# Second expert matmul in three rounded float32 terms, with the parts made on ScalarE and GpSimd

## The chip, the cores and the metric

The kernel runs on one core of a Trainium2 chip. The metric is the time of one execution on the device in microseconds (us), as a median over runs. A profiled execution leaves a page and a trace; every time in this text comes from them or from the runs.

## What is computed

A transformer layer on x of shape (16, 512, 128) in float32: layer norm, block-sparse attention and a residual, then layer norm, a mixture of four experts of which each row uses two, and a residual. The part that changes is the second matmul of the experts:

```python
h = jax.nn.gelu(jnp.einsum('nd,edh->enh', xf, w1) + b1[:, None, :], approximate=False)
y = jnp.einsum('enh,ehd->end', h, w2) + b2[:, None, :]
out = jnp.einsum('nk,nkd->nd', gates, y_sel - c_sel + c_sum[None, None, :])
```

The attention picks blocks by data: for each block of 64 queries and each head, the own block of keys and the best other one.

## The kernel before, in words

**Sizes.** B = 16 batch items, each one "batch" here. N = 512 rows, D = 128, H = 16 heads, M = 8 blocks of BS = 64 queries, E = 4 experts of C = 4 chunks of 128 hidden units, so UPS = 16 chunks per batch.

**Stages and their overlap.** The order of every engine is written out by hand; the engines meet by semaphores alone. Each batch b has a loop over m = 0 to 7, in which the attention of batch b runs. Between its steps stand the projections for batch b+1 (`a_columns`, `project`, `a_products`), the routing of batch b-1 (`c_columns`, `c_route`, `c_gates`) and the second expert matmul of batch b-2: two `c_down` per m on TensorE (L379 to L388), one between `row_max` and `shift`, one behind the next scores. After the loop come the 16 first expert matmuls `c_up` of batch b-1 (L363 to L377), each in three rounded terms (`exact`, L246 to L249, of types float32r), with the Gelu on ScalarE (L876 to L883) that fills `hid`. Behind k = 13 (`UP_SPREAD`) stands `begin(b+1)`, the scores and values of m = 0 of the next batch. Batch 15 has a tail without attention, in which 32 `c_down` and 16 `c_up` follow each other.

**An attention step m.** TensorE: `weighted(m-1)` (L322), `row_max(m)` (L306), `c_down`, `shift(m)` (L314), `scores(m+1)` (L279, line L295), `c_down`, `values(m+1)`. VectorE: `row_max` makes `nmax` (L618), for which `shift` waits; `block_max` (L603, line L609) makes `rmax` from the scores, for which `row_max` waits. ScalarE: `shift_exp` (L847), for which `weighted` waits; `values` makes `vaug` (L840).

**The selection.** At m = 6, VectorE's `a_select(b+1)` (L585 to L601) makes `index`, in ten short steps that wait for each other, the last of them L600. It stands right behind `row_max(6)` and ahead of `block_max(7)` (L764). GpSimd's `a_select` (L941, line L947) gathers with it by an indirect DMA. SP then issues `put_selected` (L1035), `put_gates`, five `place_q`, and `take_selected` (L1039, line L1044), which loads the chosen keys and values into kv. `scores(b+1, 0)` waits for its landing (`sel_in`, L285).

**GpSimd besides.** Reciprocal roots (`inverse`), `a_rows` (L938), `c_split` (L953), and `c_sum` (L967), which adds the gated experts. VectorE's `c_gated` (L705) multiplies an expert's result with its gate column; there are NG = 4 gate buffers, one for each expert, filled by SP's `take_gate` (L1056).

The f32 matmul of one `c_down` is one line, which the chip runs as two instructions:

```python
pe.wait_ge(gelued, UPS * b + n + 1)
ins = pe.matmul(dst[:], w2s[:, n, :], hid[:, n, :], start=(c == 0), stop=(c == C - 1))
```

## Time and profile before

| | us |
|---|---|
| median of 3 runs (lowest, highest) | 1009.13 (1005.77, 1011.89) |
| the profiled execution, its own time | 1008.49 |
| its span, first to last instruction | 1006.9 |
| TensorE busy (share, instructions) | 932.7 (93%, 9572) |
| VectorE busy | 552.1 (55%) |
| ScalarE busy | 460.2 (46%) |
| GpSimd busy | 172.6 (17%) |
| y_ps from hid and w2s, L386, 480 records | 260.8 busy, 629 ns each |
| first term of `exact` on w1, L247, 256 | 112.2 busy, 438 ns each |
| `block_max`, L609, 256 | 167.8 busy, 693 ns each |
| Gelu, L883, 256 | 171.5 busy, 688 ns each |

How to read it: the granted clock of TensorE is full from about 150 us on, and mostly half of it before, where the first two batches stand with gaps. Records of consecutive matmuls overlap (their ends are modelled), so a step's true length is read from start to start in the timeline and not from the mean. An average over the whole span hides what ends last in one step; the order of the steps around m = 6 and around k = 13 has to be read in the timeline.

### The profile page before, as it was taken

How to read it: one execution, taken by the hardware profiler on the slowest of the kernel's cores; microseconds unless marked ns; L12 is line 12 of the kernel's file. 1: busy time of each engine (PE TensorE's matmuls, PEld its weight loads, DVE VectorE, ACT ScalarE, POOL GpSimd, SP SyncE). 2: the span in 40 equal slices, each digit the busy share in tenths (PEclk: the TensorE clock that was granted, in tenths of full speed). 3: DMA queues.
4: the chain of work that ended last, by engine and by line, in shares of the span. 5: the costliest groups of instructions: out<-in, count | busy, mean ns of one | idle time of the engine just before them, and what ended most of it. 6: DMA issues, size and time to landing. Idle time of an engine off the chain costs nothing.

```text
span 1006.9 us, 24099 instructions
## 1 busy us (share of the span) xinstructions
PE 932.7 (93%) x9572; PEld 599.8 (60%) x9572; DVE 552.1 (55%) x1555; ACT 460.2 (46%) x740; POOL 172.6 (17%) x174
## 2 busy tenths in 40 slices
PE   3584889999999999999999999999999999999996
PEld 2362666575666666565666556566666656665652
DVE  6262645747475655747474565746575665734321
ACT  1131345363735445373635436363645436363641
POOL 3120101121212121120212121111212121110221
PEclk8575679999999999999999999999999999999998
DMA  7424052342506243352515344251615334250110
GB/s 208 115 70 120 4 142 88 109 135 72 164 14 177 63 138 103 96 147 61 164 26 150 88 123 119 76 168 36 176 38 140 99 114 119 74 159 2 54 51 14
DMA packets 96819, 101.06 MB, mean 100 GB/s; under 512 B 8744, under 2 KB 83376, under 8 KB 96688
## 3 DMA queue, kind: packets, MB, share of 16 engines
q1 hardware_dynamic: 94400, 86.89, 30.9%
q0 software_dynamic: 2304, 12.58, 3.9%
q8 instruction: 78, 1.28, 0.5%
q14 instruction: 37, 0.30, 0.1%
HBM read 48.98 MB, written 29.49 MB: 78 GB/s over the span
## 4 chain that ended last, share of the span: by engine, by line
PE 67%; DVE 17%; issue 6%; ACT 4%; SPq 3%; DMA 2%; POOL 0%; POOLq 0%; DVEq 0%
PE y_ps L386 15%; PE s_ps L295 10%; PE s_ps L318 6%; DVE rmax L609 6%; PE o_ps L329 5%; PE s_ps L247 5%; PE s_ps L249 5%; PE s_ps L248 5%; ACT hid L883 4%; SPq L1032 3%; PE v_ps L304 2%; DVE gate_cols L705 2%; PE o_ps L336 2%; PE a_ps L256 2%; PE a_ps L359 1%
## 5 line engine op out<-in xcount | busy, mean ns | idle before, releaser
L386 PE MATMUL y_ps<-hid,w2s 128*128 128x512 f32 x480 | 260.8, 629 | 0.8 <-DVE yT L705 0.2
L609 DVE TRANSPOSE_TENSOR_REDUCE rmax<-s_ps 128x16 bf16<-128x512 f32 x256 | 167.8, 693 | 165.6 <-PE s_ps L295 165.6
L847 ACT ACTIVATE prob<-s_ps 128x1024 f32<-128x1024 f32 x128 | 131.2, 1025 | 201.0 <-PE s_ps L318 200.8
L883 ACT ACTIVATE hid<-s_ps,b1s 128x512 f32<-128x512 f32 x256 | 171.5, 688 | 37.1 <-PE s_ps L249 35.4
L295 PE MATMUL s_ps<-qdiag,kv 64*128 64x512 f32 x768 | 138.2, 467 | 19.2 <-DMA kv<-kv_chosen 18.2
L840 ACT COPY vaug<-v_ps 128x128 f32<-128x128 f32 x128 | 34.0, 265 | 205.6 <-PE v_ps L304 205.6
L318 PEld LDWEIGHTS s_ps<-nmax,hone 16*128 16x128 bf16 x2048 | 69.7, 95 | 97.6 <-DVE nmax L618 96.6
L247 PE MATMUL s_ps<-xnhi,w1hi 128*128 128x512 f32 x256 | 112.2, 438 | 1.4
L967 POOL TENSOR_TENSOR yT<-yT,gate_cols 128x512 f32<-128x512 f32 x48 | 61.4, 1279 | 283.2 <-DVE gate_cols L705 282.8
L295 PEld LDWEIGHTS s_ps<-qdiag,kv 64*128 64x128 f32 x768 | 86.6, 256 | 35.2 <-issue 27.4
L248 PE MATMUL s_ps<-xnlo,w1hi 128*128 128x512 f32 x256 | 101.2, 395 | 0.0
L249 PE MATMUL s_ps<-xnhi,w1lo 128*128 128x512 f32 x256 | 101.2, 395 | 0.0
L386 PEld LDWEIGHTS y_ps<-hid,w2s 128*128 128x128 f32 x480 | 73.7, 190 | 37.7 <-issue 22.9
L318 PE MATMUL s_ps<-nmax,hone 16*128 16x64 bf16 x2048 | 85.2, 192 | 8.0 <-DVE nmax L618 5.8
L329 PE MATMUL o_ps<-prob,vaug 128*32 128x64 f32 x4096 | 88.4, 229 | 3.3 <-ACT prob L847 1.4
L329 PEld LDWEIGHTS o_ps<-prob,vaug 128*32 128x32 f32 x4096 | 67.8, 114 | 38.5 <-issue 23.9
L618 DVE TENSOR_REDUCE nmax<-v_ps 16x64 bf16<-16x256 bf16 x128 | 52.4, 409 | 69.4 <-PE v_ps L311 69.4
L247 PEld LDWEIGHTS s_ps<-xnhi,w1hi 128*128 128x128 f32 x256 | 50.1, 196 | 17.7 <-ACT hid L883 8.8
L304 PEld LDWEIGHTS v_ps<-idn,kv 128*128 128x128 f32 x128 | 24.6, 192 | 57.2 <-DVE x L637 30.7
L855 ACT COPY oT<-o_ps 128x512 f32<-128x512 f32 x64 | 37.5, 586 | 41.2 <-PE o_ps L329 40.8
L249 PEld LDWEIGHTS s_ps<-xnhi,w1lo 128*128 128x128 f32 x256 | 48.3, 189 | 11.7
L705 DVE SCALAR_TENSOR_TENSOR gate_cols<-y_ps,mT,gate_cols 128x512 f32<-128x512 f32 x45 | 32.6, 724 | 41.2 <-PE y_ps L386 41.2
(139 smaller groups left out, 1079.1 us busy)
## 6 DMA issues: line engine op xcount, KB each, us to landing
gate_cols<-gates SPq DMA_DIRECT2D x64, 256.0 KB, 5.2
kv_table<-stage SPq DMA_DIRECT2D x16, 768.0 KB, 3.9
kv<-stage SPq DMA_DIRECT2D x16, 768.0 KB, 6.2
kv_chosen<-selected SPq DMA_DIRECT2D x16, 768.0 KB, 5.3
kv<-kv_chosen SPq DMA_DIRECT2D x16, 768.0 KB, 4.9
qdiag<-qpair SPq DMA_DIRECT2D x512, 16.0 KB
xs<-in_x SPq DMA_DIRECT2D x16, 256.0 KB, 4.5
out_x<-x SPq DMA_DIRECT2D x16, 256.0 KB, 4.6
```

The costliest lines, as they stand in the source:

```text
L247: pe.matmul(dst, left_hi, right_hi, start=True, stop=False)
L248: pe.matmul(dst, left_hi, right_lo, start=False, stop=False)
L249: return pe.matmul(dst, left_lo, right_hi, start=False, stop=True)
L295: ins = pe.matmul(s_ps[i][:, half * N:(half + 1) * N].rearrange("p (h s) -> p h s", s=BS), keys, queries, start=n == 0, stop=False, skip_g ...
L318: ins = pe.matmul(s_ps[i][:, h * BS:(h + 1) * BS], hone[:, h, :], nmax[i][:], start=False, stop=True, skip_group_check=True)
L329: ins = pe.matmul(o_ps[32 * (h % HQ):32 * (h % HQ) + VW, h // HQ, i * BS:(i + 1) * BS], vaug[i][:, h, :], prob[i][:, h, :], start=True, st ...
L386: ins = pe.matmul(dst[:], w2s[:, n, :], hid[:, n, :], start=(c == 0), stop=(c == C - 1))
L609: v.tensor_reduce(rmax[m % 2][:, half * 8:(half + 1) * 8, :], s_ps[m % 2][:, half * N:(half + 1) * N].rearrange("p (a c) -> p a c", c=32), ...
L705: v.scalar_tensor_tensor(dst[:], src[:], mT[:, e:e + 1], gate_cols[i][:], ALU.add, ALU.mult).then_inc(of.free, 1)
L847: act.activation(prob[m % 2][:].rearrange("p h s -> p (h s)"), s_ps[m % 2][:], ACT.Exp, scale=SCALE).then_inc(exped, 1)
L883: act.activation(hid[:, k, :], up_ps[up_bank(k)], ACT.Gelu, bias=b1s[:, k:k + 1]).then_inc(gelued, 1)
L967: g.tensor_tensor(yT[:], yT[:], gate_cols[(E * b + e) % NG][:], ALU.add).then_inc(summed, 1)
```

## The change

The second expert matmul is computed like the first. w2 is split once into a rounded high part and a low part (`w2hi`, `w2lo`), on GpSimd, in batch 0. Each Gelu chunk gets a high part (`c_hi`: on ScalarE for n = 2 to 15, on GpSimd for n = 0, 1 and in the tail) and a low part (`c_lo`: a subtraction, on GpSimd, in the tail on VectorE). Two buffers of each serve in the loop, so a cast waits for the `c_down` two before it (`weighed_of`); in the tail eight places in `qdiag` serve. `c_down` issues three matmuls. Two gate buffers are left of four, and the gates of experts 2 and 3 are taken one batch later in SP's queue. `a_select` moves to the end of m = 6 on VectorE, and on GpSimd between two `c_lo`. The core of the diff, in the order of the file: declarations, then TensorE, VectorE, ScalarE, GpSimd (its `c_lo` uses `g`) and SP.

```diff
-        w2s = sb("w2s", [P, E * C, D])
+        w2hi, w2lo = sb("w2hi", [P, E * C, D], F32R), sb("w2lo", [P, E * C, D], F32R)
...
-        NX, N2, NG = 3, 3, E
+        NX, N2, NH, NG = 3, 3, 2, 2
...
+        hidhi, hidlo = ([sb(f"hid{part}{i}", [P, N], F32R) for i in range(NH)] for part in ("hi", "lo"))
...
-                pe.wait_ge(gelued, UPS * b + n + 1)
-                ins = pe.matmul(dst[:], w2s[:, n, :], hid[:, n, :], start=(c == 0), stop=(c == C - 1))
-                if c == C - 1:
-                    ins.then_inc(of.full, 1)
+                if b == 0 and n == 0:
+                    pe.wait_ge(w_split, SPLIT_W2)
+                pe.wait_ge(*low_of(b, n))
+                pe.matmul(dst[:], w2hi[:, n, :], hi, start=(c == 0), stop=False)
+                pe.matmul(dst[:], w2lo[:, n, :], hi, start=False, stop=False)
+                ins = pe.matmul(dst[:], w2hi[:, n, :], lo, start=False, stop=(c == C - 1))
+                ins.then_inc(of.full if c == C - 1 else weighed, 1)
...
+            def c_lo(b, n):
+                hi, lo, _ = parts_of(b, n)
+                v.wait_ge(*high_of(b, n))
+                v.tensor_tensor(lo, hid[:, n, :], hi.bitcast(F32), ALU.subtract).then_inc(lo_done, 1)
...
-                        if m == 6:
-                            tied = a_select(b + 1)
                     if b >= 1:
                         if m == 1:
                             c_route(b - 1)
...
                     if b >= 1 and m == 5:
                         c_split(b - 1)
+                    if b + 1 < B and m == 6:
+                        tied = a_select(b + 1)
                     if b >= 1 and m == 6:
                         c_gates_turned(b - 1)
...
             c_add(b - 1)
             c_gated(b, 0)
             for e in range(1, E):
+                c_los(b, e * C, (e + 1) * C)
                 c_gated(b, e)
...
+            def c_hi(b, n):
+                hi, _, was = parts_of(b, n)
+                act.wait_ge(*weighed_of(was))
+                act.copy(hi, hid[:, n, :]).then_inc(hi_cast, 1)
...
+                    if b >= 2 and m + 1 < M:
+                        c_hi(b - 2, 2 * m + 2)
                     if m in (3, 5, 7):
                         o_columns(b, (m - 3) // 2)
...
+                    if b >= 2 and m + 1 < M:
+                        c_hi(b - 2, 2 * m + 3)
                 o_copy(b, T - 1)
...
+            def c_lo(b, n):
+                hi, lo, _ = parts_of(b, n)
+                g.wait_ge(*high_of(b, n))
+                g.tensor_tensor(lo, hid[:, n, :], hi.bitcast(F32), ALU.subtract).then_inc(lo_pooled, 1)
...
+                    if b >= 2 and m in (4, 6):
+                        c_sum(b - 2, m // 2 - 1)
                     if b + 1 < B:
                         if m == 0:
                             inverse(b + 1, mv, veps, rstd, mean_done, rstd_done)
                         if m == 1:
                             a_rows(b + 1)
-                        if m == 6:
-                            a_select(b + 1)
-                    if b == 0 and m < E:
-                        split_w1(m)
+                    if b == 0:
+                        split_w(m)
+                    if b >= 2 and m + 1 < M:
+                        c_lo(b - 2, 2 * m + 2)
                     if b >= 1 and m == 5:
                         c_split(b - 1)
-                    if b >= 2 and m in (4, 6):
-                        c_sum(b - 2, m // 2 - 1)
+                    if b + 1 < B and m == 6:
+                        a_select(b + 1)
+                    if b >= 2 and m + 1 < M:
+                        c_lo(b - 2, 2 * m + 3)
                 if b >= 2:
                     c_sum(b - 2, E - 1)
+                if b >= 1:
+                    for n in range(NH):
+                        c_hi(b - 1, n)
+                    for n in range(NH):
+                        c_lo(b - 1, n)
                 inverse(b, mv2, veps2, rstd2, mean2_done, rstd2_done)
...
+                if b >= 2:
+                    take_gate(b - 2, 2)
                 if b + 1 < B:
                     place_q(b + 1, 0, range(8))
+                if b >= 2:
+                    take_gate(b - 2, 3)
                 if b + 1 < B:
                     a_v(b + 1, bank_a, bank_a)
...
```

In the tail GpSimd makes the high parts in groups (`c_his`) between its sums, and VectorE the low parts (`c_los`) between its other steps, those of an expert ahead of its `c_gated`.

## Rows read from the trace of the kernel before

**Rows 1.** Busy time of each engine in 500 to 600 us (windows view), with granted clock.

```profile
500.00:600.00 100.00, 97.85 (x1097) 61.20 (x1096) 62.81 (x174) 44.66 (x74) 17.49 (x17) 1.00 0.34 96
```

**Rows 2.** Timeline (start, length, engine, line, operation): selection chain up to the scores.

```profile
493.00 0.38 SPq L1044 DMA_DIRECT2D kv<-kv_chosen  x1
...
498.55 1.03 PE L295 MATMUL s_ps<-qdiag,kv 64*128 64x512 f32 x6
...
537.94 1.10 POOL L947 DMA_INDIRECT selected<-kv_table,index  x1 [1.79 <-DVE index L600]
...
543.69 0.59 SPq L1037 DMA_DIRECT2D kv_chosen<-selected  x1
...
550.75 0.38 SPq L1044 DMA_DIRECT2D kv<-kv_chosen  x1
...
556.37 1.03 PE L295 MATMUL s_ps<-qdiag,kv 64*128 64x512 f32 x6 [0.83 <-ACT hid L883]
```

**Rows 3.** Timeline of TensorE in the loop: two downs, and three rounded terms.

```profile
506.79 1.12 PE L386 MATMUL y_ps<-hid,w2s 128*128 128x512 f32 x2
507.84 0.64 PE L318 MATMUL s_ps<-nmax,hone 16*128 16x64 bf16 x16
...
509.91 1.13 PE L386 MATMUL y_ps<-hid,w2s 128*128 128x512 f32 x2
510.87 0.27 PE L304 MATMUL v_ps<-idn,kv 128*128 128x128 f32 x1
...
521.59 0.48 PE L247 MATMUL a_ps<-xnhi,wqkvhi 128*128 128x512 f32 x1
521.91 0.39 PE L248 MATMUL a_ps<-xnlo,wqkvhi 128*128 128x512 f32 x1
522.14 0.40 PE L249 MATMUL a_ps<-xnhi,wqkvlo 128*128 128x512 f32 x1
522.47 0.65 PE L329 MATMUL o_ps<-prob,vaug 128*32 128x64 f32 x32
```

**Rows 4.** Timeline of TensorE in the tail: the downs of two experts.

```profile
989.02 3.60 PE L386 MATMUL v_ps<-hid,w2s 128*128 128x512 f32 x8
...
992.45 3.60 PE L386 MATMUL y_ps<-hid,w2s 128*128 128x512 f32 x8
```

**Rows 5.** Timeline of TensorE, m = 6 to m = 7 of one batch.

```profile
535.59 0.64 PE L318 MATMUL s_ps<-nmax,hone 16*128 16x64 bf16 x16
536.15 1.03 PE L295 MATMUL s_ps<-qdiag,kv 64*128 64x512 f32 x6
...
541.39 0.64 PE L318 MATMUL s_ps<-nmax,hone 16*128 16x64 bf16 x16
...
543.14 0.65 PE L329 MATMUL o_ps<-prob,vaug 128*32 128x64 f32 x32
```

**Rows 6.** Groups of instructions by form: a copy on ScalarE, a subtraction on GpSimd.

```profile
L855 ACT COPY oT<-o_ps 128x512 f32<-128x512 f32 x64 | 37.5, 586 | 41.2 <-PE o_ps L329 40.8
...
L953 POOL TENSOR_TENSOR xnlo<-xn2T,xnhi 128x512 fp32r<-128x512 f32 x16 | 20.2, 1263 | 181.6 <-DVE xnhi L654 181.6
```

**Rows 7.** Timeline at m = 6, GpSimd and VectorE; last, all L591 (ns min/median/max).

```profile
534.89 1.26 POOL L953 TENSOR_TENSOR xnlo<-xn2T,xnhi 128x512 fp32r<-128x512 f32 x1 [10.89 <-DVE xnhi L654]
...
535.29 0.94 DVE L591 TENSOR_TENSOR crow<-crow,mine_of 128x64 f32<-128x64 f32 x1
...
537.44 0.21 DVE L600 TENSOR_SCALAR index<-cbest,rbase 128x1 uint32<-128x1 f32 x1
537.57 1.30 DVE L609 TRANSPOSE_TENSOR_REDUCE rmax<-s_ps 128x16 bf16<-128x512 f32 x2
...
539.25 0.29 DVE L628 TENSOR_TENSOR att<-o_ps,rden 128x128 f32<-128x128 f32 x1
...
L591 DVE TENSOR_TENSOR crow<-crow,mine_of x16: 224/934/940, 17.2 to 877.8; 128x64 f32<-128x64 f32 x16
```

**Rows 8.** Timeline of TensorE: the first scores of batch 1.

```profile
92.84 1.65 PE L295 MATMUL s_ps<-qdiag,kv 64*128 64x512 f32 x6 [9.29 <-DMA kv<-kv_chosen]
```

More of the change, by code:

```diff
@@ L243, in bank_of, with parts_of, high_of, low_of @@
             return next(of for of, _ in banks.values() if use in of.at)
+        TAIL, NT = UPS * (B - 2) + 2, 8
+        def parts_of(b, n):
+            at = UPS * b + n
+            if at < TAIL:
+                return hidhi[at % NH][:], hidlo[at % NH][:], at - NH
+            i = (at - TAIL) % NT
+            hi, lo = (q[:, i // 4, i % 4 * 2:i % 4 * 2 + 2, :].rearrange("p h s -> p (h s)") for q in qdiag)
+            return hi, lo, at - NT if at - NT >= TAIL else None
+        def high_of(b, n):
+            at = UPS * b + n
+            if at >= TAIL:
+                return hi_moved, NH * (B - 1) + at - TAIL + 1
+            return (hi_moved, NH * b + n + 1) if n < NH else (hi_cast, (UPS - NH) * b + n - NH + 1)
+        def low_of(b, n):
+            at = UPS * b + n
+            return (lo_done, at - TAIL + 1) if at >= TAIL else (lo_pooled, at + 1)
+        def weighed_of(at):
+            b, n = divmod(at, UPS)
+            if n % C == C - 1:
+                of = bank_of("down", b, n // C)
+                return of.full, of.at["down", b, n // C]
+            return weighed, at - at // C + 1
+        SPLIT_W1, SPLIT_W2 = E, 2 * E
         def tensor(pe):
@@ L799, in vector, with c_los @@
             b = B - 1
+            def c_los(b, first, last):
+                for n in range(first, last):
+                    c_lo(b, n)
+            c_los(b - 1, 2, C)
             c_split(b)
+            c_los(b - 1, C, 2 * C)
             c_gated(b - 1, 0)
@@ L982, in pool, with c_his @@
                             a_rows(b + 1)
[L983 to L986 removed]
+                    if b == 0:
+                        split_w(m)
+                    if b >= 2 and m + 1 < M:
+                        c_lo(b - 2, 2 * m + 2)
                     if b >= 1 and m == 5:
                         c_split(b - 1)
[L989 to L990 removed]
+                    if b + 1 < B and m == 6:
+                        a_select(b + 1)
+                    if b >= 2 and m + 1 < M:
+                        c_lo(b - 2, 2 * m + 3)
                 if b >= 2:
                     c_sum(b - 2, E - 1)
+                if b >= 1:
[3 more added lines that the diff above has]
+                        c_lo(b - 1, n)
                 inverse(b, mv2, veps2, rstd2, mean2_done, rstd2_done)
             b = B - 1
+            def c_his(b, first, last):
+                for n in range(first, last):
+                    c_hi(b, n)
+            c_his(b - 1, 2, C)
             c_split(b)
[L996 to L999 removed]
+            c_his(b - 1, C, 3 * C)
+            c_sum(b - 1, 1)
+            c_his(b - 1, 3 * C, 4 * C)
+            c_sum(b - 1, 2)
+            c_his(b, 0, C)
+            c_sum(b - 1, 3)
+            c_his(b, C, 3 * C)
+            c_sum(b, 1)
+            c_his(b, 3 * C, 4 * C)
+            c_sum(b, 2)
+            c_sum(b, 3)
         def sync(s):
@@ L1099, in sync @@
                 if b >= 1:
-                    for e in range(E - 1):
-                        take_gate(b - 1, e)
+                    take_gate(b - 1, 0)
                 if b + 1 < B:
@@ L1104, in sync @@
                 if b >= 1:
-                    take_gate(b - 1, E - 1)
+                    take_gate(b - 1, 1)
             b = B - 1
             store(b - 2)
+            take_gate(b - 1, 2)
+            take_gate(b - 1, 3)
             put_gates(b)
-            for e in range(E):
-                take_gate(b, e)
+            take_gate(b, 0)
+            take_gate(b, 1)
             store(b - 1)
+            take_gate(b, 2)
+            take_gate(b, 3)
             store(b)
```

54 lines of the change are left out of this document (37 added, 17 removed).

## The prediction

> **What bounds the kernel now.** I read the busy time by stretch first. In the steady state, 500 to 600 us, the clock is granted in full (1.00, the 2.4 GHz level), TensorE is busy 97.85 of 100 us, VectorE 62.81, ScalarE 44.66 and GpSimd 17.49 [rows 1]. So TensorE looks like the bound, and shorter expert matmuls look like a gain. Then I read TensorE's own timeline for what one `c_down` takes in place, and the other engines' timelines around m = 6 for what stands next to it. What the reader is to see there: between TensorE's last `shift` steps and the first scores of the next batch runs a second chain that TensorE's busy time hides: block selection on VectorE (`a_select`), gather on GpSimd, `put_selected` and `take_selected` on SP, landing, `scores(b+1, 0)`. In the batch at 537 us it even ends last: the scores at 556.37 stand behind 0.83 us of idle, 5.62 us after `take_selected` was issued at 550.75 [rows 2]. The view names ScalarE's L883 as releaser, but that gelu (k = 13) isn't what this step waits for; the landing of kv is. In the batch before, 493.00 to 498.55 is 5.55 us, without idle [rows 2]. So this chain has between 0 and some 0.6 us of slack; I take 0.4.
>
> **Part 1, three terms in place of one f32 matmul.** A `c_down` in the loop takes 1.05 us to the `shift` behind it (506.79 to 507.84) and 0.96 us to the transpose behind it (509.91 to 510.87) [rows 3]. Three rounded terms of the same shape (128 columns of weights, 512 moving) take 0.32 + 0.23 + 0.33 = 0.88 us, from 521.59 to the next step at 522.47 [rows 3]. So I take 0.88 for the new `c_down`: 0.17 and 0.08 less, nearly 2 us for the 16 of a batch. Back to back, four f32 downs take 3.43 us (989.02 to 992.45) [rows 4], and four triples at 0.23 a term some 2.8, so up to 0.6 for an expert in the tail. Not all of it counts: in m = 2, 4 and 6 VectorE, not the down, sets when `shift` starts, and in m = 7 the exp sets when `weighted` starts: 543.14, 1.75 us after `shift` at 541.39 [rows 5]. I take 1.2 us per batch from the scores of a batch to its `shift(6)`, with ends 0 and 1.9. Batches 2 to 14, 13 of them, are where it meets the selection chain.
>
> **Part 2, the casts on ScalarE.** 14 `c_hi` per batch. The nearest rows are copies and casts of 128x512 from PSUM at 0.586 us [rows 6]: 8.2 us per batch of 57.8 (the scores at 498.55 to those at 556.37 [rows 2]). ScalarE idles over half the time, and each `c_hi` stands where it used to wait for TensorE: behind an exp (that one is over 1.75 us after `shift` starts [rows 5], so the cast some 2.3 us after it) or behind `values`. Its own wait, for the down two before, is satisfied by then. Queued behind it are `attT` and `vaug`; both have a few tenths of a microsecond left. I cost it at 0, at most 0.2 for each of m = 3, 5 (0.4 per batch).
>
> **Part 3, the subtractions on GpSimd.** 16 `c_lo` at 1.263 us (nearest row, the same subtraction in `c_split` [rows 6]) plus two copies, for which no more than that: at most 22.7 us per batch on top of some 10 [rows 1], so 33 of 57.8. Per m that is 2.5 us in some 5.8 (`shift(6)` to `shift(7)` [rows 5]), and a buffer's round (down, cast 0.58, subtraction 1.26) stays under one m. The tight ones by this count are `c_lo(2)`, because exp(0) waits for a table load, and 4, 12, 13 and 14: ready within 0.3 us of their use. Cost 0, at most 0.5 per batch. The exception is `c_lo(15)`, in part 4.
>
> **Part 4, `a_select` moved, on both engines.** This sets the sign. On VectorE it stood behind `row_max(6)` and ends now at 537.65 (537.44 + 0.21), 2.06 us after `shift(6)` at 535.59 [rows 5, 7]. It is moved behind `block_max(7)`, `o_project` and `o_rows`. `block_max(7)` starts now at 537.57, held back by the selection; scores(7) run 536.15 to 537.18 [rows 5], so it can start at about 537.23, 0.34 earlier. The work from its start to the end of L628 is 1.97 us (537.57 to 539.54) [rows 7], which gives 539.2. With one short step ahead of it (0.2 us, my estimate) L591 starts near 539.4, and from the end of L591 to that of L600 it is 1.42 us. L591 takes 0.224 us when alone and 0.934 as median: it ends with `c_split` on GpSimd (534.89 + 1.26 = 536.15, L591 at 536.23) [rows 7]. After the change `c_lo(14)`, started behind `c_lo(13)` and `c_sum`, runs to about 540.05 and holds it the same way. So the index is there at about 541.55, 5.96 us after `shift(6)`: 3.9 us later (3.4 if L591 finds the port free). Everything in the chain follows one to one: gather, 543.69 for `put_selected`, 550.75 for `take_selected`, since SP waits for the gather with nothing else to do and the five `place_q` DMAs between the two are still to be issued behind it. 3.9 less 0.4 of slack: the next batch's scores start 3.5 us later after `shift(6)`.
>
> Beside this, `row_max(7)` on VectorE now queues behind `a_select` and the gate copy: `shift(7)` moves from +5.80 to about +6.6 us. And on GpSimd `c_lo(15)` queues behind the gather, which waits for the index: index + 0.29 + 1.10 [rows 2] + 1.26 is +8.6; `down(15)` follows, and `weighted(7)` behind it starts at +9.5, where it starts at +7.55 now [rows 5]. That is 1.9 us, but inside the 3.5.
>
> The Trainium skill (SBUF — State Buffer, "SBUF: two separate sides") calls the port pair that VectorE and GpSimd share an exclusive lock, held for a whole instruction, against a VectorE instruction with two SBUF inputs. On L591 the trace agrees, 0.224 against 0.934 us. Its page GPSIMD Engine Reference ("Engine selection") speaks against part 3: two-input elementwise work belongs on VectorE, about twice as fast. The sum does without either.
>
> **Part 5, two gate buffers, start and tail.** The takes of gates 2 and 3 move to the next batch's queue on SP, ahead of `place_q` and of `a_v`; what they wait for (`c_gated(0)` and the first `c_sum`) is there by m = 4, before `a_v` can go. Cost 0 to 0.3. Batch 0: TensorE waits 9.29 us for that chain, until 92.84 [rows 8], so nothing of the 3.9 is slack, and the scores ahead of the moved selection are slower, 1.65 us there against 1.03 [rows 5, 8]: 3.9 + 0.6 = +4.5. Batch 1 has more slack and no `c_lo`: +2 (0 to 3.5). The split of w2 on GpSimd (four more pairs, at most 2 x 1.263 us each) ends before anything needs it. In the tail of 32 downs, TensorE gains up to 0.55 per expert, but the high parts go to GpSimd (between 0.6, as ScalarE needs, and 1.26 each) and the low parts to VectorE (some 0.65), in series with `c_gated` in VectorE's queue: the last three experts come out level with now (by my estimate 2.9 for the downs, 0.7 for `c_gated` and 2.5 for four subtractions, where [rows 4] have 3.43 for the downs alone and one expert's gate hidden behind the next). I take +1, from -4 to +5.
>
> **The sum.** 13 x (3.5 - 1.2) = 30; batches 0 and 1 add 6.5; the tail 1: +37.5 on the profiled execution's 1008.5 us (span 1006.9), so 1046. The median of the runs shown is 1009.1, 0.6 higher, well inside the range.
>
> **The rivals.** (a) The chain of DMAs isn't what ends last: the index is later, but SP or the landings give the time back. Then the delay of `shift(7)` and `down(15)` is left, 1.9 us: 13 x (1.9 - 1.2) = 9, with 4.5 + 1 + 1 it is 1024. For it speaks that I have the slack from two batches only; against it the 0.83 us of idle in one of them. (b) The shared port costs more: GpSimd's back-to-back instructions win against a waiting VectorE in `c_gates` (L680, L685 of m = 3), so that `nmax` waits for a whole `c_sum`, and in the tail casts and subtractions alternate. Up to 1.2 us per batch and 3 in the tail: 1065. The rule of the Trainium skill named above would lead here, if the port went to the queue that is ready first. (c) The other side: TensorE's instructions set the end, and each of the 256 downs gives back 0.13 us in the loop and up to 0.17 in the tail: 256 x 0.15 = 38, so 970. It decides if the chain behind the index has more than about 3.5 us of slack and `c_lo(15)` comes in time; 97.85 of 100 us busy speaks for it, the idle before the scores against. (d) The gain and the moves cancel, within 0.5% of now. That the three terms cost as much as one f32 matmul is excluded by the same form in [rows 3].
>
> **How the numbers follow.** Forecast 0.57 (its own range 1030 to 1060: the ends of parts 1 and 4, 13 x (3.0 - 1.7) and 13 x (3.9 - 0.6), with the start and the tail), (a) 0.15, (b) 0.16, (c) 0.08, (d) 0.04. The range reaches to (a) and (b): 1018 to 1066. A measurement of this kernel tells about 0.5%, 5 us, from no change. Faster by more 0.08, within 0.04, slower by more 0.88.
>
> **What would show it.** L600's end some 6 us after `shift(6)` where it is 2.06; TensorE idle before `scores(b+1, 0)` in every batch with kv<-kv_chosen as releaser, and before `down(15)` with GpSimd; a period between batches of some 59 us where it is 57; triples at 0.7 to 0.9 us; L591 still near 0.9. I am wrong if TensorE has no idle there, if the index comes within 4 us, or if the clock falls below 1.00 in the steady state.

## The result, and the profile after

| | before | after |
|---|---|---|
| median (lowest, highest), us | 1009.19 (1005.77, 1011.89) | 1056.4 (1054.42, 1060.87) |
| ratio, with its 95% interval | | 1.0476 (1.043 to 1.0522), slower |
| the profiled execution, its span, us | 1008.49, 1006.9 | 1056.25, 1054.4 |
| first scores of batch 1 | 92.84 | 97.00 |
| from there to the first scores of batch 2 | 64.2 | 63.5 |
| 13 batches, scores of batch 2 to scores of batch 15 | 741.0 (57.0 each) | 780.3 (60.0 each) |
| scores of batch 15 to the end | 108.9 | 113.6 |

The change costs 47 us. Of these 4.2 come ahead of batch 1, -0.7 in batch 1, 39.3 in the 13 batches and 4.7 behind them. A second profiled execution of the same kernel gave 93.76, 66.4, 779.3 and 116.2: between these two the ends of the program differ by 2 to 3 us, the 13 batches by one. A third execution of the same loop, in the kernel of "The tail's casts on ScalarE" below, has 774.9 us for them, so they too differ by up to 5.

The page of after: busy time and share of each engine, then TensorE's granted clock in 40 slices.

```profile
PE 918.2 (87%) x9828; PEld 659.0 (63%) x9828; DVE 593.0 (56%) x1585; ACT 561.1 (53%) x936; POOL 511.0 (48%) x468
...
PEclk9675799999899999999999999989999999989998
```

TensorE has 14.5 us less to do (932.7 before) and the kernel is 47 us longer: the loss is no added work of TensorE (what a lower clock adds is inside the 918.2). In the stretch of [rows 1], 500 to 600 us (windows view: busy time of PE, PEld, DVE, ACT, POOL, then clock, DMA share, GB/s), it is busy 91.93 us where it was 97.85, and the clock isn't full any more, 0.98:

```profile
500.00:600.00 100.00, 91.93 (x978) 66.52 (x978) 57.35 (x165) 61.58 (x103) 52.28 (x48) 0.98 0.37 102
```

The groups of the page that are new (count, busy us, mean ns, idle before):

```profile
L1048 POOL TENSOR_TENSOR hidlo<-hid,hidhi 128x512 fp32r<-128x512 f32 x226 | 288.3, 1281 | 168.0 <-ACT hidhi L937 167.6
...
L427 PE MATMUL y_ps<-hidhi,w2hi 128*128 128x512 f32 x226 | 113.6, 503 | 22.5 <-POOL hidlo L1048 19.2
L937 ACT CAST hidhi<-hid 128x512 fp32r<-128x512 f32 x196 | 120.8, 616 | 0.0
```

A cast on ScalarE takes 0.616 us and a subtraction on GpSimd 1.281 us, where [rows 6] had 0.586 and 1.263.

**The selection chain**, timeline of after, one batch whose `shift(6)` starts at 498.94. It answers to [rows 2, 7].

```profile
502.13 1.26 POOL L1048 TENSOR_TENSOR hidlo<-hid,hidhi 128x512 fp32r<-128x512 f32 x1
...
502.72 0.75 DVE L633 TENSOR_TENSOR crow<-crow,mine_of 128x64 f32<-128x64 f32 x1
...
504.67 0.21 DVE L642 TENSOR_SCALAR index<-cbest,rbase 128x1 uint32<-128x1 f32 x1
...
505.17 1.10 POOL L1015 DMA_INDIRECT selected<-kv_table,index  x1 [1.78 <-DVE index L642]
...
510.25 0.58 SPq L1147 DMA_DIRECT2D kv_chosen<-selected  x1
...
516.95 0.38 SPq L1154 DMA_DIRECT2D kv<-kv_chosen  x1
...
581.78 1.03 PE L333 MATMUL s_ps<-qdiag,kv 64*128 64x512 f32 x6 [1.46 <-DMA kv<-kv_chosen]
```

The index ends at 504.88, 5.94 us after `shift(6)` (+2.06 before). The step in which VectorE multiplies by `mine_of` is held until `c_lo(14)` ends on GpSimd. The load of kv is issued some 18 us after `shift(6)`, the scores follow 5.4 us later. In the batch of the last row, which starts `shift(6)` at 558.32, TensorE stands idle for them for 1.46 us, and the releaser is the landing. Such an idle, 1.4 to 1.7 us, stands in four of the 13 batches. In the other nine TensorE comes as late or later by itself, which is the next point.

**The clock.** Timeline of TensorE in the same batch, from the end of `down(14)`, and the windows view of the same stretch (length, TensorE's busy time, granted clock, DMA share, GB/s):

```profile
504.28 0.40 PE L429 MATMUL y_ps<-hidlo,w2hi 128*128 128x512 f32 x1
505.46 0.64 PE L356 MATMUL s_ps<-nmax,hone 16*128 16x64 bf16 x16 [0.79 <-DVE nmax L660]
...
507.63 0.67 PE L427 MATMUL y_ps<-hidhi,w2hi 128*128 128x512 f32 x1 [1.28 <-POOL hidlo L1048]
508.10 0.63 PE L428 MATMUL y_ps<-hidhi,w2lo 128*128 128x512 f32 x1
```

```profile
505.50:506.40 0.90, 0.85 (x17) 1.00 0.11 18
506.40:507.63 1.23, 0.00 (x0) 1.00 0.69 83
507.63:511.00 3.37, 3.37 (x38) 0.52 0.52 213
```

TensorE pauses 0.79 us ahead of `shift(7)` and 1.28 us ahead of `down(15)`, which waits for its low part. Then the granted clock is at its lower level (1.2 of 2.4 GHz) for 3.4 us: a term takes 0.63 to 0.67 us in place of 0.40 to 0.50. Such a stretch stands behind `shift(7)` in 9 of the 13 batches, and those are the nine without idle ahead of the scores. In five it is 3.4 us long, and the scores start at +23.4, where they also start behind an idle; in four (batches 3, 6, 10 and 14) it is 6.8 us long, and they start at +24.7 to +24.8. In batches 2 and 5 the clock is full in m = 7, and falls behind the idle ahead of the scores (1.50 and 1.69 us) instead, 0.72 in the 6 us behind it, so that the next `shift(6)` is 1.3 us late; behind the other two idles, of 1.46 and 1.38 us, it stays full. The periods follow: 60.7 to 62.0 us in four batches, 59.4 to 59.7 in nine.

**The tail.** VectorE's low parts and TensorE's first terms of the next expert, timeline; last, the low parts of a later expert and a sum on GpSimd:

```profile
1000.62 4.11 DVE L739 TENSOR_TENSOR qdiag<-hid,qdiag 128x512 fp32r<-128x512 f32 x4 [1.97 <-POOL qdiag L1043]
...
1001.83 0.47 PE L427 MATMUL v_ps<-qdiag,w2hi 128*128 128x512 f32 x1 [0.82 <-DVE qdiag L739]
1002.76 0.50 PE L427 MATMUL v_ps<-qdiag,w2hi 128*128 128x512 f32 x1
1003.77 0.50 PE L427 MATMUL v_ps<-qdiag,w2hi 128*128 128x512 f32 x1
...
1014.49 2.48 DVE L739 TENSOR_TENSOR qdiag<-hid,qdiag 128x512 fp32r<-128x512 f32 x4
...
1014.64 3.48 POOL L1055 TENSOR_TENSOR yT<-yT,gate_cols 128x512 f32<-128x512 f32 x1 [1.49 <-DVE gate_cols L752]
```

Four subtractions take 4.11 us beside GpSimd's casts, and the downs come every 1.02 us. At 1014.49, with GpSimd not casting, four take 2.48, and it is GpSimd's sum that waits: 3.48 us where it takes 1.28. From the routing transposes of batch 15 to the end it is 57.6 us, 51.9 before.

### The profile page after: what moved, and what is told of

Its sections match the earlier page's. It is cut to its first block, busy times and chain, and to the rows that moved or that the text cites. A ratio compares the mean times of both kernels' runs of the same rounds, so it can differ in the third digit from the quotient of the medians.

```text
span 1054.4 us, 25191 instructions
## 1 busy us (share of the span) xinstructions
PE 918.2 (87%) x9828; PEld 659.0 (63%) x9828; DVE 593.0 (56%) x1585; ACT 561.1 (53%) x936; POOL 511.0 (48%) x468
## 4 chain that ended last, share of the span: by engine, by line
PE 42%; issue 14%; DVE 12%; POOL 11%; ACT 8%; DMA 7%; SPq 5%; POOLq 0%; DVEq 0%; ACTq 0%
POOL hidlo L1048 7%; PE s_ps L333 7%; PE s_ps L356 4%; SPq L1142 4%; PE y_ps L427 4%; PE s_ps L285 4%; DVE rmax L651 3%; DMA kv<-kv_chosen 3%; ACT hid L947 3%; PE s_ps L287 3%; DMA selected<-kv_table,index 3%; PE s_ps L286 3%; PE o_ps L367 3%; PE y_ps L428 2%; PE y_ps L429 2%
## 5 line engine op out<-in xcount | busy, mean ns | idle before, releaser
L1048 POOL TENSOR_TENSOR hidlo<-hid,hidhi 128x512 fp32r<-128x512 f32 x226 | 288.3, 1281 | 168.0 <-ACT hidhi L937 167.6
L427 PE MATMUL y_ps<-hidhi,w2hi 128*128 128x512 f32 x226 | 113.6, 503 | 22.5 <-POOL hidlo L1048 19.2
L937 ACT CAST hidhi<-hid 128x512 fp32r<-128x512 f32 x196 | 120.8, 616 | 0.0
L285 PE MATMUL s_ps<-xnhi,w1hi 128*128 128x512 f32 x256 | 116.1, 454 | 1.4
L286 PE MATMUL s_ps<-xnlo,w1hi 128*128 128x512 f32 x256 | 104.9, 410 | 0.0
L999 POOL TENSOR_SCALAR veps<-mv 128x4 f32<-128x4 f32 x32 | 7.3, 227 | 175.4 <-DVE mv L576 175.4
L428 PE MATMUL y_ps<-hidhi,w2lo 128*128 128x512 f32 x226 | 91.3, 404 | 0.0
L429 PE MATMUL y_ps<-hidlo,w2hi 128*128 128x512 f32 x226 | 91.0, 403 | 0.0
L660 DVE TENSOR_REDUCE nmax<-v_ps 16x64 bf16<-16x256 bf16 x128 | 52.2, 408 | 59.7 <-PE v_ps L349 59.7
L1055 POOL TENSOR_TENSOR yT<-yT,gate_cols 128x512 f32<-128x512 f32 x48 | 65.0, 1355 | 42.4 <-DVE gate_cols L752 42.4
L427 PEld LDWEIGHTS y_ps<-hidhi,w2hi 128*128 128x128 f32 x226 | 42.9, 190 | 56.9 <-POOL hidlo L1048 24.4
```

Source lines behind the costliest of these rows:

```text
L285: pe.matmul(dst, left_hi, right_hi, start=True, stop=False)
L286: pe.matmul(dst, left_hi, right_lo, start=False, stop=False)
L427: pe.matmul(dst[:], w2hi[:, n, :], hi, start=(c == 0), stop=False)
L937: act.copy(hi, hid[:, n, :]).then_inc(hi_cast, 1)
L1048: g.tensor_tensor(lo, hid[:, n, :], hi.bitcast(F32), ALU.subtract).then_inc(lo_pooled, 1)
```

## The experiments

Each ran on one chip with the kernel before. The move alone, the move undone, low part 15 ahead of the gather and the three terms alone ran beside 1007.99 us; the pauses filled, the selection clear, the tail's casts and the first kernel of "Together" beside 1006.9; SP's queue, the second kernel of "Together" and the two repeats beside 1007.92. "+" is time after the start of `shift(6)`; "period" is from scores to scores of the profiled execution.

### The move of the selection alone

The kernel before with one edit on VectorE:

```diff
-                        if m == 6:
-                            tied = a_select(b + 1)
...
                         c_split(b - 1)
+                    if b + 1 < B and m == 6:
+                        tied = a_select(b + 1)
```

> The kernel before, with one edit: VectorE's selection stands at the end of m = 6, as in the changed kernel; f32 downs, no casts, no subtractions. My theory (the later selection costs most of the time, through the chain of gather and DMAs): the index some 5.6 us after shift(6) where it was 2.05, the next scores at about +23.0 to +23.4 where they were +19.9, with idle released by kv<-kv_chosen, so about +3.2 us for each of 13 batches and +4 at the start: about 1053. Rival (the load on GpSimd and ScalarE makes the change slow, the move matters only with them): within 10 us of before, below 1020.

Measured: 1068.51 us, ratio 1.0605 (1.0574 to 1.0637), slower than the whole change. The index ends at +5.42 (the step with `mine_of` finds GpSimd free, 0.23 us), the kv load goes out at +17.6, the scores start at +22.5 to +23.4 with TensorE idle in all 13 batches. Timeline and windows of one such place (windows: length, busy PE, PEld, DVE, ACT, POOL, clock, DMA share, GB/s):

```profile
525.82 1.39 PE L295 MATMUL s_ps<-qdiag,kv 64*128 64x512 f32 x6 [1.80 <-DMA kv<-kv_chosen]
```

```profile
523.40:525.80 2.40, 0.62 (x3) 0.19 (x2) 0.00 (x0) 0.98 (x2) 0.00 (x0) 1.00 1.02 324
525.80:530.00 4.20, 4.18 (x14) 2.68 (x15) 1.31 (x2) 0.95 (x2) 0.00 (x0) 0.59 0.56 177
```

So the move alone makes the slowdown, and the chain of DMAs behind the index ends last. The theory has the chain right and was 15 us short: in all 13 batches the clock falls behind this idle of 1.6 to 2.5 us, 0.59 over 4.2 us here, and from the scores to the next `shift(6)` it is then 38.5 us, 37.0 before. Of the 4.25 us that a period is longer (61.25), 1.45 are the clock's and the rest the chain's. In m = 7 the clock is full in all 13: `down(15)` is an f32 matmul of finished rows here and doesn't wait for a low part.

### The move undone

The changed kernel with VectorE's `a_select` back behind `row_max(6)`; GpSimd's order as changed.

```diff
+                        if m == 6:
+                            tied = a_select(b + 1)
...
-                    if b + 1 < B and m == 6:
-                        tied = a_select(b + 1)
```

> The changed kernel, with one edit: VectorE's selection stands behind row_max(6) again, as before; GpSimd's gather stays between the low parts 14 and 15. My theory: the index at about +2.1 to +3.4 us after shift(6), the gather behind low part 14 at about +4.5, the scores at +19.9 to +21.5; a period of 56 to 57.3 us where the changed kernel has 60.0, no wait of 1.3 us for low part 15, no fall of the clock in m = 7: about 1056 - 13 x 3.3 - 4 = 1010. Rival (load on GpSimd): still above 1040.

Measured: 1038.17 us, ratio 1.0292 (1.0233 to 1.035), between the two expectations; both are wrong in size. The move is worth 18 us, not 46, and some 30 remain. Timeline of VectorE and GpSimd in one batch, `shift(6)` at 487.38:

```profile
487.24 0.95 DVE L633 TENSOR_TENSOR crow<-crow,mine_of 128x64 f32<-128x64 f32 x1
...
488.74 0.64 DVE L636 TENSOR_TENSOR cties<-cown,ctop 128x8 f32<-128x8 f32 x1
...
489.49 1.13 DVE L638 TENSOR_TENSOR crank<-cties,rank 128x8 f32<-128x8 f32 x1
```

```profile
489.32 1.28 POOL L1055 TENSOR_TENSOR yT<-yT,gate_cols 128x512 f32<-128x512 f32 x1
490.56 1.26 POOL L1048 TENSOR_TENSOR hidlo<-hid,hidhi 128x512 fp32r<-128x512 f32 x1
491.99 1.10 POOL L1015 DMA_INDIRECT selected<-kv_table,index  x1 [0.17 <-issue]
```

Three steps of the selection combine two tiles of SBUF element by element (it has nine steps, not ten), and each ends only when GpSimd's instruction ends: 0.95, 0.64 and 1.13 us, where two of them take 0.17 and 0.16 alone, on 8 elements a partition. The last step, at 490.85, runs beside `c_lo(14)` and takes 0.21 us as always. The index comes at +3.69 in place of +2.06, the gather stands behind `c_lo(14)` besides, `shift(7)` comes at +7.3 in place of +5.8. TensorE pauses once, for 2.0 us:

```profile
492.52 0.38 PE L342 MATMUL v_ps<-idn,kv 128*128 128x128 f32 x1 [1.99 <-DVE x L679]
```

This pause stands in all 13 batches, and the clock falls behind it in five. So GpSimd's new instructions, by the steps that they hold, cost more than its move adds to them. In the changed kernel the two hide each other in part: the moved selection meets only one of them.

### The low part of chunk 15 ahead of the gather

```diff
-                    if b + 1 < B and m == 6:
-                        a_select(b + 1)
                     if b >= 2 and m + 1 < M:
                         c_lo(b - 2, 2 * m + 3)
+                    if b + 1 < B and m == 6:
+                        a_select(b + 1)
```

> The changed kernel, with one edit: on GpSimd low part 15 stands ahead of the gather, so it doesn't wait for the index, and the gather is not later. Theory A (the chain of DMAs ends last, at +23.4): down(15) starts 2 us earlier, TensorE's wait moves to the scores, the period falls only by what the half clock costs, some 0.6 us of 60: 1045 to 1052. Theory B (the wait for low part 15, and the half clock behind it, ends last): the period falls by 2 to 3 us: 1020 to 1030. Whether the granted clock stays at 1.00 shows if the 1.3 us of idle ahead of down(15) made it fall.

Measured: 1065.82 us, ratio 1.0591 (1.0547 to 1.0635). Both theories expected a gain, and there is none: `down(15)` no longer waits, and the kernel is 1.1% slower than the changed one. `c_lo(15)` now holds a second step of the selection, the index comes at +6.48, 0.54 later, and TensorE idles ahead of the scores in all batches (the view names kv in 11 of 13 and the Gelu in two). Timeline of VectorE and TensorE, `shift(6)` at 498.51:

```profile
503.58 0.70 DVE L636 TENSOR_TENSOR cties<-cown,ctop 128x8 f32<-128x8 f32 x1
...
505.56 0.64 PE L356 MATMUL s_ps<-nmax,hone 16*128 16x64 bf16 x16 [1.32 <-DVE nmax L660]
...
506.21 0.63 PE L427 MATMUL y_ps<-hidhi,w2hi 128*128 128x512 f32 x1
```

TensorE's wait for `c_lo(15)` was inside the wait for the transfer, as part 4 of the prediction has it. The clock doesn't need that wait to fall: with one pause of 1.32 us ahead of `shift(7)` it is low in m = 7 of 12 of the 13 batches.

### The three terms alone

The kernel before with w2 split and the three terms in each `c_down`, whose moving rows are one constant tile; no high or low parts of `hid` are made, so the experts' results are left out.

```diff
-                ins = pe.matmul(dst[:], w2s[:, n, :], hid[:, n, :], start=(c == 0), stop=(c == C - 1))
+                rows = fixed[:]
...
+                pe.matmul(dst[:], w2hi[:, n, :], rows, start=(c == 0), stop=False)
+                pe.matmul(dst[:], w2lo[:, n, :], rows, start=False, stop=False)
+                ins = pe.matmul(dst[:], w2hi[:, n, :], rows, start=False, stop=(c == C - 1))
```

> The kernel before with three float32r terms in each down, and nothing else of the change: no high and low parts are made, the moving rows of all three terms are a fixed buffer, so the experts' result is left out; w2 is split as in the change. My theory: the down takes 0.88 us, the time from scores to shift(6) falls from 37.0 to about 36.0, in the tail each expert 0.6 us: 1009 - 13 x 1.1 - 4 = 991. Rival (TensorE sets the end everywhere): 256 x 0.15 = 38 us less, 971. Second rival (nothing comes through, since other chains end last): 1005 or more.

Measured: 987.59 us, ratio 0.9799 (0.9771 to 0.9828). From the scores to the next `shift(6)` it is 35.79 us in place of 37.02, 1.23 less: part 1 took 1.2. The period is 55.95, and from the routing transposes to the end it is 47.4 us in place of 51.9.

### SP's queue: the load of kv ahead of five places of q

```diff
-                    place_q(b + 1, 1, range(4, 9))
                     take_selected(b + 1)
+                    place_q(b + 1, 1, range(4, 9))
```

> The changed kernel, with the load of the chosen keys and values ahead of the five places of q in SP's queue; nothing else is moved. With the same order in the kernel with everything together the load was issued at +12.7 to +14.5 us after shift(6), in place of +14.0 to +14.9. Theory: the transfer that begins with the gather ends last in the changed kernel, in nine of its 13 batches (periods of 59.4 us with TensorE idle for 1.4 to 1.7 us ahead of the scores), so that each of these gains 1.2 to 1.5 us, and the four in which the clock halves gain nothing: 1056 - 12 = 1044 us (1040 to 1050). Rival: TensorE's own work ends last and the idle ahead of the scores would show up elsewhere: 1056 us, within 3.

Measured: 1045.36 us, ratio 1.0369 (1.0348 to 1.0391), 11 us less than the changed kernel beside it (1.0473). The load goes out at +16.4 in place of +18.0. The theory holds where the clock does: three batches have a period of 57.8 to 57.9 us, their scores at +21.9 without idle, 1.5 us earlier than in the changed kernel. In nine batches the clock is low in m = 7, and TensorE comes at +23.4 to +24.8 whatever the transfer does; one batch stands between, at 58.7. The number expected, 1044, is met partly by luck: the theory had nine batches with the transfer last, where the trace of the changed kernel has four, and three gain the 1.5 us. The 13 batches took 770.8 us, 9.5 less than in the changed kernel's first execution, and part of that is that the clock fell behind the scores in none of them.

### The pauses filled

```diff
                         c_down(b - 2, 2 * m)
+                        if m == 7:
+                            fill(3)
...
+                        if m == 7:
+                            fill(5)
                         c_down(b - 2, 2 * m + 1)
...
+            def fill(count):
+                for _ in range(count):
+                    pe.matmul(y_ps[:], zeros[:], w2hi[:, 0:4, :].rearrange("p c d -> p (c d)"), start=False, stop=False)
```

> The changed kernel, with three extra TensorE instructions in m = 7 ahead of shift(7) and five ahead of c_down of chunk 15. They multiply by a tile of zeros and add it to the open sum, so nothing else changes; each is 128x512 in float32r, 0.23 us by the spacing of the terms in the tail, and they lie in stretches in which TensorE waits for others (0.79 and 1.28 us). Theory: in the batches that lose more than the forecast (four of 13 by 1.4 to 2.6 us, 7.9 us together) the granted clock halves because TensorE stood still twice in m = 6 to 7; with the pauses filled the clock stays at 1.00 and the periods are 59.4 us all through: 1056 - 8 = 1048 us (1045 to 1051). Rival: the clock has nothing to do with these pauses, or is of no weight for what ends last: 1056 us or a little more (1055 to 1060), with rows at half clock in m = 7 as before.

Measured: 1052.23 us, ratio 1.0458 (1.0434 to 1.0482). Timeline of TensorE, and the windows behind it (length, busy time, clock, DMA share, GB/s):

```profile
500.69 0.86 PE L435 MATMUL y_ps<-w2hi,zeros 128*128 128x512 f32 x3
501.66 0.64 PE L357 MATMUL s_ps<-nmax,hone 16*128 16x64 bf16 x16
...
502.31 1.41 PE L435 MATMUL y_ps<-w2hi,zeros 128*128 128x512 f32 x5
503.85 0.50 PE L428 MATMUL y_ps<-hidhi,w2hi 128*128 128x512 f32 x1
```

```profile
503.00:505.00 2.00, 1.87 (x25) 1.00 0.89 252
505.00:507.00 2.00, 2.00 (x37) 1.00 0.34 141
```

`shift(7)` comes at the same +6.52, and from there to the scores the clock is 1.00 in all 13 batches, where it was lower in 9 of 13. Now the transfer shows in every batch: TensorE idles 0.8 to 1.7 us ahead of the scores, which start at +22.9 to +23.8. The 13 batches take 771.6 us in place of 780.3, as expected, but in this execution the tail took 4 us more, and the whole time is above the 1045 to 1051 of the theory.

I ran both once more, on one chip:

> The changed kernel itself once more, beside these on the same chip. Theory, with the clock: about one batch in three loses 1.3 to 2.6 us to half clock in m = 7, which ones differing from execution to execution: 1052 to 1060 us, and 3 to 9 us above the 1052 of the kernel with its pauses filled. Rival: the same as that kernel, within 1 us.

> The changed kernel with the zero-weight instructions in the pauses of m = 7, once more, beside the changed kernel on one chip. Theory: 3 to 9 us faster than the changed kernel, with every batch from the fourth on at 58.8 to 59.5 us. Rival: no difference, within 1 us.

Measured: 1056.57 us (1.0473, 1.0451 to 1.0495) for the changed kernel and 1052.92 us (1.0435, 1.0411 to 1.0458) with the pauses filled. The gain of 3.7 us is at the low end of what was expected, and the intervals just meet, so the whole time shows it weakly. That the clock in m = 7 hangs on the pauses the traces show well: low in 8 of 13 batches against 0 of 13. Its price they show less well: 779.3 against 773.1 us for the 13 batches, where the same loop without the filling took 774.9 in the third execution. Not every batch kept to the 58.8 to 59.5 us expected either: four of them took 59.6 to 61.1. What is left at half clock with the pauses filled stands behind idles ahead of the scores of 2.39 and 1.61 us, which were not filled; behind one of 1.60 us in the same execution it stayed full.

### The selection kept clear of GpSimd

The changed kernel, with the selection back behind `row_max(6)` on VectorE, and on GpSimd:

```diff
-                    if b >= 2 and m in (4, 6):
+                    if b >= 2 and m == 4:
                         c_sum(b - 2, m // 2 - 1)
+                    if b + 1 < B and m == 6:
+                        a_select(b + 1)
...
-                    if b >= 1 and m == 5:
+                    if b >= 1 and m == 6:
                         c_split(b - 1)
-                    if b + 1 < B and m == 6:
-                        a_select(b + 1)
                     if b >= 2 and m + 1 < M:
                         c_lo(b - 2, 2 * m + 3)
+                    if b >= 2 and m == 6:
+                        c_sum(b - 2, m // 2 - 1)
```

> The changed kernel, with the selection back behind row_max(6) on VectorE, and GpSimd kept clear of it: its order is c_lo(12), c_lo(13), then the gather, c_lo(14), c_split, c_lo(15) and the sum of expert 2. All the work is there. In the kernel with VectorE's move alone undone three of the ten steps were held beside c_split, a low part and the sum (0.95, 0.64 and 1.13 us), so that the index was at +3.7 us after shift(6) and shift(7) at +7.3. Theory: what was left of the slowdown there is GpSimd's instructions beside the selection; with them away the index is at +2.1 to +2.5, shift(7) at about +6, the next scores at +20 to +20.5, the period 56 to 56.5 us: 13 batches give back 2 to 3 us each of the 1038 and the pauses that lower the clock go: 1000 to 1012 us. Rival: the loss comes from GpSimd's load as such (low parts hold VectorE everywhere in the loop, casts hold ScalarE), and its order only moves it: 1028 us or more.

Measured: 1005.82 us, ratio 1.0009 (0.9981 to 1.0037). All of the work is there, and 47 us are gone. Timeline, `shift(6)` at 472.25:

```profile
473.38 0.17 DVE L636 TENSOR_TENSOR cties<-cown,ctop 128x8 f32<-128x8 f32 x1
...
473.66 0.16 DVE L638 TENSOR_TENSOR crank<-cties,rank 128x8 f32<-128x8 f32 x1
...
474.55 1.10 POOL L1015 DMA_INDIRECT selected<-kv_table,index  x1 [1.78 <-DVE index L642]
...
479.47 0.50 PE L427 MATMUL y_ps<-hidhi,w2hi 128*128 128x512 f32 x1 [0.65 <-POOL hidlo L1048]
```

Of the steps only the one with `mine_of` is still held, by `c_lo(13)` (0.73 us; 0.93 in the kernel before). The index is at +2.01, all 13 batches have a period of 56.4, TensorE doesn't idle ahead of the scores, and the clock is full from `shift(7)` to the scores and behind them in all 13. The rival, that GpSimd's load costs wherever it stands, falls: what costs is where its instructions stand.

### The tail's casts on ScalarE

The changed kernel, in whose tail ScalarE makes all high parts but two, between its Gelus and copies; GpSimd keeps the sums.

```diff
             c_columns(B - 1)
+            for n in range(C, 3 * C):
+                c_hi(B - 2, n)
             c_logits(B - 1)
+            for n in range(3 * C, 4 * C):
+                c_hi(B - 2, n)
             for k in range(UPS):
                 c_up(B - 1, k)
+                if k == 2 * C - 1 or k == 3 * C - 1:
+                    for n in range((k // C - 1) * C, k // C * C):
+                        c_hi(B - 1, n)
+            for n in range(2 * C, 4 * C):
+                c_hi(B - 1, n)
```

> The changed kernel, with the high parts of the tail made on ScalarE, all but two of them, in place of GpSimd; VectorE makes the low parts in the same order. Theory: in the tail the c_down are spaced 1.02 us because GpSimd's cast and VectorE's subtraction hold each other by turns; alone the subtraction takes 0.62 us a piece. Then the spacing falls to 0.70, and the waits of 0.82, 0.67 and 0.66 us go; the waits of 1.53 us behind a c_gated stay. Four groups gain about 1.4 us each: 1056 - 5 = 1051 us (1049 to 1053). Rival: VectorE's own order (a c_gated ahead of each group) sets the tail, and the casts fit beside it: 1056 us, within 1.

Measured: 1049.27 us, ratio 1.0412 (1.0387 to 1.0436), 6 us below the changed kernel by the ratios. The groups of VectorE's low parts and ScalarE's casts (count, busy us, mean ns):

```profile
L741 DVE TENSOR_TENSOR qdiag<-hid,qdiag 128x512 fp32r<-128x512 f32 x30 | 24.2, 864 | 0.1
...
L944 ACT CAST qdiag<-hid 128x512 fp32r<-128x512 f32 x28 | 15.1, 621 | 0.0
```

In the first two experts that had waited, the downs come every 0.70 us where they came every 1.02, as expected. In the last two the waits of 1.53 us stay, as expected, and those of 0.66, which was not; behind them the clock is low for 3.4 us each, and the downs come every 1.28 to 1.45. In the tail of the changed kernel the same waits stand and the clock is full there. So in the trace only 2 us of the gain stand in the tail (55.4 us from the routing transposes to the end, 57.6 and 58.9 in two executions of the changed kernel): its clock was 0.81 from 1020 to 1030 us and 0.61 from there to the end, and the 13 batches happened to take 775 us. So the cause, casts and subtractions in turns, is shown, its price only to between 2 and 6 us.

### Together, and c_split last

First all of it: the selection clear, SP's queue, the tail's casts, and VectorE's low parts of the last batch one `c_gated` earlier. Then the same with `c_split` behind `c_lo(15)`. The edits that are new, on VectorE in the tail (first kernel) and on GpSimd (second):

```diff
-            c_gated(b, 0)
-            for e in range(1, E):
-                c_los(b, e * C, (e + 1) * C)
+            for e in range(E):
+                if e + 1 < E:
+                    c_los(b, (e + 1) * C, (e + 2) * C)
                 c_gated(b, e)
...
-                    if b >= 1 and m == 6:
-                        c_split(b - 1)
                     if b >= 2 and m + 1 < M:
                         c_lo(b - 2, 2 * m + 3)
+                    if b >= 1 and m == 6:
+                        c_split(b - 1)
```

> All of it together: the selection clear of GpSimd, the loads of the chosen keys ahead of five places of q in SP's queue, the tail's high parts on ScalarE, and on VectorE each group of low parts of the last batch one c_gated earlier. Theory: as e8, less 0.5 us per batch for SP's queue where the transfer ends last (up to 7), less 5 us for the casts and 2 x 1.4 us for the order: 990 to 1000 us, faster than the kernel before. The three terms with a fixed operand alone gave 988 us, which bounds it. Rival: the transfer behind the gather, at 18 us from the index to the scores, is last in every batch, and nothing is had from SP's queue: 1000 to 1008 us.

Measured: 998.07 us, ratio 0.9914 (0.9888 to 0.9939). The period is 56.43 as without SP's edit: nothing is had from SP's queue, as the rival said, but not for its reason. The load goes out at +12.6 to +14.5, TensorE has no idle ahead of the scores, and so it is TensorE, not the transfer, that sets the end there. The gain over the kernel before it stands in the tail, 48.7 us from the routing transposes where that had 59.2.

> The kernel with everything together, with c_split behind c_lo(15) on GpSimd in place of ahead of it. In that one the low part of chunk 15 starts 1.24 us after its high part is there, beside c_split, and TensorE waits 0.65 us for it ahead of its c_down. Theory: weighted(7) comes at +7.5 in place of +8.1, the scores at +19.9 in place of +20.5, and 13 batches take 55.8 us each in place of 56.4: 998 - 8 = 990 us (986 to 994), as far as the three terms alone went (988). Rival: the transfer is last by then, so the scores stay at +20.4: 997 us or more.

Measured: 981.84 us, ratio 0.9749 (0.9727 to 0.9771): 2.5% faster than the kernel before, and better than expected. Stretch 500 to 600 us, and TensorE at m = 7 and at the scores:

```profile
500.00:600.00 100.00, 96.60 (x1067) 69.39 (x1068) 61.91 (x173) 63.79 (x109) 55.90 (x49) 1.00 0.39 113
```

```profile
471.36 0.48 PE L429 MATMUL y_ps<-hidhi,w2hi 128*128 128x512 f32 x1
...
484.80 1.03 PE L335 MATMUL s_ps<-qdiag,kv 64*128 64x512 f32 x6
```

`down(15)` starts without a wait, `weighted(7)` at +7.43, the scores at +19.77, the period is 55.74, 1.3 less than before. GpSimd is busy 56 of 100 us and ScalarE 64, both more than in the changed kernel, beside a full clock. The profiled executions of the two, 994.06 and 984.68, differ by 9.4 us, of which 8.9 stand in the 13 batches (8 expected). The medians differ by 16; where the other 7 are can't be read from one trace of each.

## Why the prediction was right, and where it was off

The sign, the mechanism and the range held: 1056.4 was measured, 1046 forecast, 1018 to 1066 the range. Of the 10 us between, the 13 batches have some 9 and the tail nearly 4, and the start took 3 back. By its steps:

- **Part 1** held. The three terms gave 1.23 us per batch alone and 1.06 in the changed kernel (35.96 from the scores to the next `shift(6)`, 37.02 before), 1.2 forecast.
- **Part 2** held: a cast takes 0.616 us and the trace shows GpSimd waiting for it, and TensorE only for the low part behind it.
- **Part 3** held as a cost of 0 outside m = 6 and 7. It missed that the subtractions matter through whom they hold: undoing the move left 30 us, which no step of mine names. Part 4 had one step of the selection held; behind `row_max(6)` GpSimd holds three, and the gather waits for `c_lo(14)` besides.
- **Part 4** held almost to the tenth: index +5.94 (5.96 forecast), `shift(7)` +6.52 (6.6), `weighted(7)` +9.58 where the clock was full (9.5), scores +23.4 or a little more where the clock was full and they waited for the landing (23.4). The period is 59.4 us in the usual batch, 2.4 above the mean of before; 2.3 was the forecast.
- **The clock** is the term that was missing in the sum. I had named a clock below 1.00 as a sign of being wrong, and then cost it at nothing. It fell in 9 of 13 batches in m = 7 and in two more behind the scores; in this execution four batches lost 1.3 to 2.6 us more than the other nine, 8 us together, which is the difference between 31 and 39.3. How much it takes differs from execution to execution: with the same loop the 13 batches took 774.9 to 780.3. It also hid the idle that I had named as the sign to look for: ahead of the scores it stands in four batches, not in all.
- **The start** was put at +6.5 and measured at +3.5: batch 0 +4.2 (4.5 forecast), batch 1 -0.7 (2 forecast). The second execution has the sum at +3.1.
- **The tail** was mis-sized: +1 forecast, +4.7 measured, +7.3 in the second execution. The attention of batch 15 gains 0.9, the rest loses 5.7. I had the casts and subtractions run at their lone times beside each other; they hold each other in turns. That was in rival (b), at 3 us.

**The rivals.** (a), the DMAs not last: excluded by the move alone, with idle released by kv in all 13 batches, and by the idle ahead of the scores in every batch once the pauses were filled (kv in 10 of 13 by the view, the Gelu in three, as in the prediction's [rows 2]); in the changed kernel itself the transfer and the slowed TensorE come within tenths of each other in most batches. (b), the port: its place in the loop was wrong, VectorE isn't passed over in `c_gates`, where its step of 0.74 us (0.85 before) ends with one GpSimd instruction and before the next starts; in the tail it was right. (c), TensorE sets the end at 970: not in this order; in the order of the last kernel, where TensorE does set the end, it is 982. (d): no.

The Trainium skill's rule of the exclusive lock (SBUF — State Buffer, "SBUF: two separate sides") is borne out by every held step here, 0.95, 0.64 and 1.13 us. The Trainium skill's rule in GPSIMD Engine Reference, "Engine selection", that two-input work is about twice as fast on VectorE, agrees in its figure, 1.28 us on GpSimd against 0.62 on VectorE (four in 2.48); but the kernel at 981.84 us has 226 such subtractions on GpSimd. They are off the path there.

## What to carry to other kernels

Before a helper engine gets work, list the short dependent steps on the other engine that read two operands from SBUF, and place the new instructions so that none runs beside them: here the same work cost 47 us in one order and gained 26 in another (with the tail's casts on ScalarE). Don't move a chain with a long transfer behind it to make room; what follows it is moved by as much, and its slack is read from the wait ahead of the consumer, batch by batch. And when a forecast contains new pauses of TensorE, price the clock behind them, from rows at half clock.

## What the hardware showed that I had not expected

- Two pauses of 0.79 and 1.28 us, 0.9 us of work between them, were followed by a stretch at half clock (3.4 us in the one shown) in 9 of 13 batches, 8 of 13 in a second execution, and in none of 26 with the pauses filled. One pause of 1.32 us ahead of `shift(7)` was followed by one in 12 of 13 batches (low part 15 first), and one of 2.0 us in m = 6 in 5 of 13 (the move undone). Ahead of the scores, pauses of 1.6 to 2.5 us were followed by one in all 13 batches of the kernel with the move alone, where it cost 1.45 us; in the kernel with its pauses filled one of 1.74 us was, and 12 of up to 1.58 us were not. So the length of the pause alone doesn't tell it, and what does is not shown here.
- A VectorE step on 128x8 elements, 0.16 us alone, took 1.13 us beside one sum of 128x512 on GpSimd, and another 0.64 beside a subtraction. In the timelines here it ended with that instruction, also where others followed back to back: the waiting VectorE came in between two GpSimd instructions. The other way round it was not so in the tail: GpSimd's sum, waiting beside four subtractions of VectorE back to back, ended only 1.15 us after the last of them (3.48 us in place of 1.28).
- Casts on GpSimd and subtractions on VectorE in turns came one of each every 1.02 us; alone a cast takes 0.61 us and a subtraction 0.62.
